# Fused gated cross-attention and routed feed-forward on one core: another order of the first loads and splits, and matmuls without a use where TensorE waits

## The reference

```python
x = x + tanh(g_xattn) * xattn(layernorm(x), ctx, ctx, Wq, Wk, Wv, Wo, bo)   # 16 heads of 16, causal
x = x + tanh(g_ffn) * ffn(layernorm(x), controller, f1, bias, f2)
# xattn: Q = q@Wq.T; K = k@Wk.T; V = v@Wv.T; softmax(mask(Q K^T)/4) V; @Wo.T + bo
# ffn: tokens in groups of 32; logits = grouped @ controller, 32 experts x 4 sets;
#      each (expert, set) takes the one token of its group with the highest logit;
#      relu(token @ f1 + bias) @ f2, and the result goes back to the token it came from
```

## Time and profile before

| | us |
|---|---|
| median of 3 runs | 309.36 |
| lowest, highest | 309.05, 312.26 |
| the profiled execution's own time | 311.98 |
| its span, first to last instruction | 310.3 |
| PE, DVE, ACT, POOL busy in the span | 243.7, 197.7, 168.3, 124.1 |
| mean granted TensorE clock | 0.912 |

### The profile page before, as it was taken

How to read it: one execution, slowest core, us unless ns; L and a number is a source line. 1 busy time by engine, 2 the same in 40 slices (tenths; PEclk the granted TensorE clock), 3 DMA queues, 4 the chain that set the end, 5 groups by cost and what they waited for, 6 DMA issues and landing times.

```text
span 310.3 us, 8572 instructions
## 1 busy us (share of the span) xinstructions
PE 243.7 (79%) x3426; PEld 193.9 (62%) x3426; DVE 197.7 (64%) x433; ACT 168.3 (54%) x345; POOL 124.1 (40%) x230
## 2 busy tenths in 40 slices
PE   0617163798989899898888878698998888789995
PEld 0617052776768687686666656476766777677773
DVE  4574755496859779485777799989995443412222
ACT  1521243485877768485757645336785443334553
POOL 4140233557776767675556665624541000000000
PEclk9985765599999999799989999979999999859999
DMA  6929985647677675738551000049940000001211
GB/s 175 212 92 185 288 167 100 142 109 163 149 178 139 150 162 133 162 65 182 116 138 23 4 4 5 0 145 396 388 161 2 3 4 4 4 2 68 69 68 68
DMA packets 21961, 35.87 MB, mean 116 GB/s; under 512 B 2915, under 2 KB 15779, under 8 KB 20387
## 3 DMA queue, kind: packets, MB, share of 16 engines
q1 hardware_dynamic: 21059, 34.01, 43.1%
q10 hardware_dynamic: 864, 1.33, 1.9%
HBM read 26.65 MB, written 8.39 MB: 113 GB/s over the span
## 4 chain that ended last, share of the span: by engine, by line
PE 27%; POOL 24%; issue 23%; DVE 13%; DMA 7%; ACT 4%; SPq 1%; POOLq 0%; DVEq 0%
POOL pT L377 9%; PE banks L763 7%; PE banks L735 6%; DMA cT<-in_ctxT_dram 6%; PE banks L472 4%; PE banks L772 3%; POOL xs L371 3%; POOL qp L362 3%; POOL kp L362 2%; DVE permb L1144 2%; POOL onl L401 2%; DVE rsum L1099 2%; DVE gmax L1130 1%; PE banks L581 1%; DVE lt L1125 1%
## 5 line engine op out<-in xcount | busy, mean ns | idle before, releaser
L1091 DVE TENSOR_REDUCE nmax<-banks 128x4 f32<-128x512 f32 x64 | 43.7, 685 | 37.5 <-PE banks L535 37.5
L377 POOL TENSOR_SCALAR_AFFINE_SELECT pT<-pT 128x512 f32<-128x512 f32 x64 | 40.7, 637 | 45.4 <-ACT pT L866 45.3
L866 ACT ACTIVATE pT<-banks 128x512 f32<-128x512 f32 x64 | 37.6, 590 | 8.2 <-PE banks L552 7.8
L871 ACT ACTIVATE banks<-cb 128x512 f32<-128x512 bf16 x62 | 37.0, 596 | 5.6 <-DVE nmax L1091 5.5
L581 PE MATMUL banks<-pT,va 128*32 128x128 f32 x512 | 27.7, 289 | 0.8 <-POOL pT L377 0.8
L535 PE MATMUL banks<-kst,qst 96*128 96x128 bf16 x256 | 26.7, 231 | 1.7 <-ACT banks L871 1.4
L1099 DVE RECIPROCAL rsum<-banks 128x256 f32<-128x256 f32 x16 | 28.0, 1748 | 0.0
L552 PE MATMUL banks<-qst,kst 99*128 99x128 bf16 x256 | 25.9, 225 | 1.0 <-ACT pT L866 1.0
L581 PE MATMUL banks<-pT,ones 128*32 128x128 f32 x512 | 26.4, 279 | 0.0
L763 PEld LDWEIGHTS banks<-cf,routed 128*128 128x128 f32 x128 | 21.1, 250 | 7.2 <-issue 6.2
L985 ACT ACTIVATE ys<-banks 128x1024 f32<-128x1024 f32 x16 | 16.7, 1046 | 16.0 <-PE banks L763 16.0
(11 more groups left out here) (115 smaller groups left out, 633.4 us busy)
## 6 DMA issues: line engine op xcount, KB each, us to landing
wx<-in_wexp_dram SPq DMA_DIRECT2D x32, 256.5 KB, 6.8
q_rows<-qp SPq DMA_DIRECT2D x8, 384.0 KB, 2.5
k_rows<-kp SPq DMA_DIRECT2D x8, 384.0 KB, 4.9
qst<-q_rows SPq DMA_DIRECT2D x8, 384.0 KB, 4.7
kst<-k_rows SPq DMA_DIRECT2D x8, 384.0 KB, 4.8
cT<-in_ctxT_dram SPq DMA_DIRECT2D x8, 256.0 KB, 6.7
qst<-q_rows SPq DMA_DIRECT2D x8, 256.0 KB, 5.5
kst<-k_rows SPq DMA_DIRECT2D x8, 256.0 KB, 5.6
```

The source lines that it names most:

```text
L377: pool.affine_select(p, p, [[0, HC], [1, P]], ALU.is_ge, 0.0, base=0, channel_multiplier=-1)\
L866: act.activation(pT[:, n % PR, :], BT[n % 2], ACT.Exp, scale=float(D) ** -0.5).then_inc(p_ready, 1)
L871: act.activation(BS[n % 2], causal, ACT.Copy).then_inc(mask_placed, 1)
L1091: dve.tensor_reduce(nmax[:, b % 2, :].rearrange("p (e j o) -> p e o j", e=2, o=KH)[:, e, o], BS[n % 2].rearrange("p (j t) -> p j t", j=HC) ...
```

## The change

It changes the order of the fill on all engines, and adds 25 matmuls whose result is never read.

- SP: x of 0-1 and 2-3 first, then context pairs 0, 1 and 2 (pair 2 waits for its buffer, that is for `context_low(0)`), V (from ACT's queue), x of 4-7, the shift rows; keys ahead of queries; gates (from ACT's queue) and context pair 3 behind the stacks of pair 0; keep and stack of pair 1; then x of 8-11, WO (from ACT's queue), x of 12-15, the rest of the constants and the controller.
- ACT: loads the identity alone, K and Q; high part of K ahead of the context; context pair 2 and V ahead of `xT_high(1)`; WO's high part in slot 3 of the loop.
- POOL: low part of K (new `weight_low_by_dim`); all three `context_low` ahead of the first `low_part`; WO's low part in slot 4; the controller's copy in slot 56.
- DVE: statistics and `rstd` of four sequences at once; no low part of K; the low part of query pair 0 (new `q_low_first`).
- PE: `keep_warm(9)` ahead of the first transposes and `keep_warm(16)` ahead of the loop.

```diff
--- before.py
+++ after.py
@@ -45,7 +45,7 @@
 LA = 10
 SLOTS_N = 4 * NB + 17
 PARTS = 3
-XL = ((0, 2), (2, 4), (4, 8), (8, 16))
+XL = ((0, 2), (2, 4), (4, 8), (8, 12), (12, 16))
 SROWS = 6 * D
 TROWS = SROWS + PARTS
 STACKS = 4
@@ -145,6 +145,7 @@
 
 
         x_loaded = [sem(f"x_loaded{i}") for i in range(len(XL))]
+        ident_loaded = sem("ident_loaded")
         consts_loaded = sem("consts_loaded")
         masks_ready = sem("masks_ready")
         small_loaded = sem("small_loaded")
@@ -295,24 +296,29 @@
                 stack(kst, k_rows, g, ((0, 3), (1, 3), (2, 3)), k_kept, k_stacked[g % STACKS])
 
             load_x(0)
+            load_x(1)
             load_context(0)
+            load_context(1)
+            load_context(2)
+            sp.dma_start(w[:, V], wattn[:, V]).then_inc(w_loaded[V], 16)
+            load_x(2)
             sp.wait_ge(shift_ready, 1)
             sp.dma_start(kst[SROWS:TROWS].rearrange("p s h b c -> p (s h) (b c)"),
                          shift[:, None, :].to_broadcast([PARTS, STACKS * H, 2 * P])).then_inc(shift_stacked, 16)
-            load_x(1)
-            load_context(1)
-            load_x(2)
+            keep_k(0)
             keep_q(0)
-            keep_k(0)
+            stack_k(0)
             stack_q(0)
-            stack_k(0)
+            sp.dma_start(gb[:, :], gbo).then_inc(gates_loaded, 16)
+            load_context(3)
+            keep_k(1)
+            keep_q(1)
+            stack_k(1)
+            stack_q(1)
             load_x(3)
-            load_context(2)
-            keep_q(1)
-            keep_k(1)
-            stack_q(1)
-            stack_k(1)
-            load_context(3)
+            sp.dma_start(w[:, WO], wattn[:, WO]).then_inc(w_loaded[WO], 16)
+            load_x(4)
+            sp.dma_start(cf[:, P:], constf[:, P:]).then_inc(consts_loaded, 16)
             sp.dma_start(ctrl_in[:, :, :], ctrl).then_inc(small_loaded, 16)
             for g in range(NG2 + 1):
                 if g >= 1:
@@ -365,6 +371,14 @@
                 pool.wait_ge(w_high, m + 1)
                 pool.tensor_tensor(wl[:, m], w[:, m], wh[:, m].bitcast(F32), ALU.subtract).then_inc(w_low[m], 1)
 
+            def weight_low_by_dim(m):
+                pool.wait_ge(w_high, 1)
+                for j in range(2 * KH):
+                    out, high = [t[:, m].rearrange("p k (o d h) -> p (k o) d h", o=KH, d=D)[:, j] for t in (wl, wh)]
+                    last = pool.tensor_tensor(out, w[:, m].rearrange("p k (o h d) -> p (k o) d h", o=KH, d=D)[:, j],
+                                              high.bitcast(F32), ALU.subtract)
+                last.then_inc(w_low[m], 1)
+
             def bias_x(b):
 
                 pool.wait_ge(xn_ready, b + 1)
@@ -411,20 +425,15 @@
                 pool.wait_ge(perm_ready, b + 1)
                 pool.tensor_copy(permT[:, b, :], pc[:, k, :]).then_inc(permT_kept, 1)
 
-            pool.wait_ge(consts_loaded, 16)
+            pool.wait_ge(ident_loaded, 16)
             pool.tensor_copy(identb, ident).then_inc(masks_ready, 1)
-            context_low(0)
-            low_part(qp, 2, qr, 1, 0, qm_ready, ql_ready)
+            weight_low_by_dim(K)
+            for g in range(3):
+                context_low(g)
             low_part(kp, 0, kr, 1, 0, km_ready, kl_ready)
-            context_low(1)
+            weight_low(V)
+            low_part(kp, 0, kr, 1, 1, km_ready, kl_ready)
             low_part(qp, 2, qr, 1, 1, qm_ready, ql_ready)
-            low_part(kp, 0, kr, 1, 1, km_ready, kl_ready)
-            context_low(2)
-            weight_low(V)
-            pool.wait_ge(small_loaded, 16)
-            pool.tensor_copy(ctrl_sb[:, :, :].rearrange("p h (s e) -> p h s e", s=NS),
-                             ctrl_in[:, :, :].rearrange("p h (e s) -> p h s e", s=NS)).then_inc(ctrl_ready, 1)
-            weight_low(WO)
             for n in range(SLOTS_N):
                 s, g = n % 8, n // 8
                 if s % 4 == 0 and 0 <= n // 4 - 1 < NB:
@@ -437,10 +446,16 @@
                     low_part(qp, 2, qr, 1, g + 1, qm_ready, ql_ready)
                 if s == 3 and g + 2 < NG2:
                     low_part(kp, 0, kr, 1, g + 2, km_ready, kl_ready)
+                if n == 4:
+                    weight_low(WO)
                 if s % 4 == 2 and n // 4 < NB:
                     if n == 2:
                         pool.wait_ge(bo_ready, 1)
                     bias_x(n // 4)
+                if n == CH - 8:
+                    pool.wait_ge(small_loaded, 16)
+                    pool.tensor_copy(ctrl_sb[:, :, :].rearrange("p h (s e) -> p h s e", s=NS),
+                                     ctrl_in[:, :, :].rearrange("p h (e s) -> p h s e", s=NS)).then_inc(ctrl_ready, 1)
                 if s == 5 and g + 3 < NG2:
                     context_low(g + 3)
                 if n in (CH + 7, CH + 9, CH + 11):
@@ -608,7 +623,14 @@
                     pe.wait_ge(pm_ready, b - 1)
                 pe.transpose(BP[b % 2][:, 0:P], pc[:, b % 2, :], ident).then_inc(pm_done, 1)
 
-            pe.wait_ge(consts_loaded, 16)
+            def keep_warm(times):
+
+                for _ in range(times):
+                    pe.matmul(bank[1], identb, causal, start=True, stop=True)
+
+            pe.wait_ge(masks_ready, 3)
+            keep_warm(9)
+            pe.wait_ge(ident_loaded, 16)
             transpose_x(0, BB)
             pe.wait_ge(w_low[K], 1)
             for o in range(KH):
@@ -622,7 +644,7 @@
             for o in range(KH):
                 project_q(1, o, bank[2])
 
-            pe.wait_ge(masks_ready, 3)
+            keep_warm(16)
             pe.wait_ge(ones_ready, 2)
             pe.wait_ge(shift_stacked, 16)
             for n in range(SLOTS_N):
@@ -785,15 +807,12 @@
 
         @block.scalar
         def _(act):
-            act.dma_start(cf[:, :], constf).then_inc(consts_loaded, 16)
-            for i in range(2):
+            act.dma_start(ident, constf[:, 0:P]).then_inc(ident_loaded, 16)
+            for i in (K, Q):
                 act.dma_start(w[:, i], wattn[:, i]).then_inc(w_loaded[i], 16)
 
             act.wait_ge(act_warm, 1)
             act.activation(warm[:, :], warm[:, :], ACT.Exp)
-            for i in range(2, 4):
-                act.dma_start(w[:, i], wattn[:, i]).then_inc(w_loaded[i], 16)
-            act.dma_start(gb[:, :], gbo).then_inc(gates_loaded, 16)
 
             def context_high(g):
                 act.wait_ge(ctx_loaded[g % 2], 16 * (g // 2 + 1))
@@ -894,25 +913,24 @@
                 act.activation(rT[:, :, :], bank[0][:, 0:E].rearrange("p (h t) -> p h t", h=KH), ACT.Copy)\
                     .then_inc(rT_ready, 1)
 
+            weight_high(K)
             context_high(0)
-            weight_high(K)
             weight_high(Q)
             xT_high(0, BB)
+            context_high(1)
             k_high(0)
+            k_mid(0)
             q_high(0, bank[4])
             q_mid(0)
-            k_mid(0)
-            context_high(1)
+            context_high(2)
+            weight_high(V)
             xT_high(1, bank[3])
             k_high(1, bank[5])
+            k_mid(1)
             q_high(1, bank[2])
             q_mid(1)
-            k_mid(1)
-            context_high(2)
-            weight_high(V)
             act.wait_ge(gates_loaded, 16)
             act.activation(tg[:, :], gates_sb[:, :], ACT.Tanh).then_inc(tanh_ready, 1)
-            weight_high(WO)
             for n in range(SLOTS_N):
                 s, g = n % 8, n // 8
                 if 1 <= n < CH - 1:
@@ -931,6 +949,8 @@
                     k_high(g + 2)
                 if s == 2 and g + 2 < NG2:
                     k_mid(g + 2)
+                if n == 3:
+                    weight_high(WO)
                 if s == 4 and g + 3 < NG2:
                     context_high(g + 3)
                 if s == 6 and g + 2 < NG2:
@@ -1077,6 +1097,10 @@
                     dve.wait_ge(ql_ready, g)
                 dve.tensor_tensor(qr[:, :], of, qp[:, 0, :], ALU.subtract).then_inc(qr_ready, 1)
 
+            def q_low_first():
+                dve.wait_ge(qm_ready, 1)
+                dve.tensor_tensor(qp[:, 2, :], qr[:, :], qp[:, 1, :], ALU.subtract).then_inc(ql_ready, 1)
+
             def xT_low(g, of=BA):
 
                 dve.wait_ge(xTh_ready, g + 1)
@@ -1144,17 +1168,16 @@
                 dve.tensor_tensor(permb[:, b % 2, :, :], bank[(2, 7)[b % 2]][:, None, 0:P].to_broadcast([P, NG, P]),
                                   groupmask[:, :, None].to_broadcast([P, NG, P]), ALU.mult).then_inc(pm_ready, 1)
 
-            rstd_rows(0, 2)
+            rstd_rows(0, 4)
             normalize_x(0)
             normalize_x(1)
-            weight_low(K)
             weight_low(Q)
             xT_low(0, BB)
+            normalize_x(2)
+            normalize_x(3)
             k_rest(0)
             q_rest(0, bank[4])
-            rstd_rows(2, 4)
-            normalize_x(2)
-            normalize_x(3)
+            q_low_first()
             xT_low(1, bank[3])
```

(1 more changed line is left out.)

## The result

| us | before | changed |
|---|---|---|
| median (range, runs) | 310.77 (309.05 to 312.26, 4) | **319.74** (315.78 to 322.7, 4) |
| profiled execution, span | 311.98, 310.3 | 320.74, 319.0 |
| mean granted clock | 0.912 | 0.875 |

The ratio is 1.0251, 95% interval 1.0166 to 1.0337. Forecast were 309.0 and a range of 305.4 to 312.6, so the time lies 7 us outside.

The account below looks back on a forecast made before the run. It took the loss to be in the fill, in waits for DMAs and POOL. 4.7 us in, 5.03 out, 5.63 out, some 6 in, and the clock's share: slot 8 0.3 earlier, 309.0 against 309.36, range 305.4 to 312.6.

Parts of the forecast that it names:

- Part 1: Fill up to the first scores: the stacks of pair 0 land at 39.0 us against 34.3, 4.7 us later.
- Part 2: From the stacks of pair 0 to slot 8: WO lands at 54.5, slot 8 starts at 61.1 us against 61.42.
- Part 3: The rest: both keep_warm bursts lie in PE's waits and work added to the loop is hidden, 0 us.
- I give it 0: Clock effect of keep_warm(16): none carried to slot 0 or through the wait for WO; 0 us, bounds 0 and -1.9.
- POOL's loop: 0: WO's low part and the controller's copy enter POOL's loop, which has 5.9 us free of 18: 0, at most 0.7.
- from slot 8 ... the change does almost nothing there: From slot 8, first matmul at 61.42 us, the loop repeats and the change does almost nothing.
- a loop from slot 8 to the experts that is off by over 1 us: Sign of being wrong: the loop from slot 8 to the experts, taken as unchanged, longer or shorter by over 1 us.
- Faster: Rival, fill: x of 2-3 lands at 7.0 and the chain runs in POOL's gaps; 305.9 us, chance 0.20.
- Slower by POOL's tiles: Rival, fill: POOL's strided tiles of Wk cost up to 1.27 us each, all 2.8 later; 312.1 us, chance 0.15.
- Clock kept up: Rival, `spread_max(0)` to slot 8: the clock stays up, 18 matmuls take 1.9 us less; 307.1 us, chance 0.08.

## Why the prediction was wrong, and where it was right

**Part 1, late stacks: right, 1.4 us short.** Forecast 39.0, measured 40.40. X of 2-3 landed at 8.66 (8.27), and from the first stack's issue to the last landing it took 11.43 (11.45). K landed at 8.21, not 6.75; its tiles on POOL took 1.93, not 1.6. The rows were ready at 15.15, not 13.8: besides the 1.11 that one tiny instruction took under POOL's 1.26 (1.1 forecast), four more took 0.37 to 0.48 under POOL's four tiles of 0.48, where others of their size took 0.16. Each of the five ends 0.02 to 0.03 us behind the end of a POOL instruction. The Trainium skill, "SBUF — State Buffer", section "Who interferes with whom", states that a DVE instruction with two SBUF inputs contends with a GpSimd instruction that reads SBUF. The rows of L1031, L1033 and L1039 agree; L1029 and L1036 have one tile as input and waited as long, which that section has only for a two-port mode of DVE, and no run shows whether they were in it. I had let the loss act once instead of five times.

**Part 2, the queue behind the stacks: right, and WO 2.2 us short.** WO forecast at 54.5, read at 56.75 behind a wait of 8.43 (6 to 8). The stacks of pair 1 were issued 1 us late (42.08 for 41.1), and the queue from there to x of 8-11 took 13.9 us instead of 12.6. `spread_max(0)` came at 58.46 (56.2), slot 8 at 62.99 (61.1; my own terms add up to 61.2), 4.53 later and not 5.33, since the clock rose at 62. These are mis-sized terms, 1.9 us in all. The reorder alone, which is the change without its matmuls, came out 0.4 above before by the medians of one batch; the forecast for the whole was 0.3 below.

**Part 3: the step that failed.** "keep_warm(9) ... costs nothing" and "I give it 0" are right where I looked: the nine run from 4.57 to 7.98, the sixteen from 27.39 on, both inside waits, and the clock at slot 0 is 0.54. That no clock is carried there holds for this order, with 9.6 us between the sixteen and the scores; on the kernel before, without that gap, it was 0.84. "POOL's loop: 0" is right as well (12.15 of 18 us, before 12.14). But the cost was set to nothing for the whole kernel, with "from slot 8 ... the change does almost nothing there", and in the experts' stage, 180 us behind them, the 25 matmuls cost 8 us: with them 319.74, without 311.64 (in one batch 320.67 with 25 of 32 columns, and 311.64). They do it by the place to which 50 more instructions push the code behind, not by their work: 25 of 32 columns cost as much, 128 nothing that is told. Among its signs of being wrong the prediction has only a loop from slot 8 to the experts that is off by over 1 us. That loop was right (175.68 us, before 176.63); the experts' stage it didn't name at all.

**The rivals.** Faster: transposes came at 15.29, not before 12. Slower by POOL's tiles: 0.48 each, under the 0.7 from which it decides. Clock kept up: no. So the right sign stood in one rival and the right mechanism in none.

**Shown and not shown.** Shown is that the count of added instructions decides, by the place of the code behind (0, 25 and 118 on several fills, 128 on one), that with 25 the clock falls 7 to 12 us into the stage and otherwise after 26 or more, and that ahead of every fall inside the stage stands a second burst that took longer. That PE's stops are waits for a piece of code rests on their timing, 1.2 to 1.7 us behind a packet's end in 33 of 33; no run delays a packet. Argued only is that the longer burst itself drops the clock: the fall follows it after 0.5 us in one kernel and after 6.3 to 7.0 in five, so something else has a part in when it falls. Only instructions ahead of the stage were added, all of them matmuls; another kind on PE, or one on another engine, was not tried. How much of the spread of before's runs (304 to 315) is this clock was not looked into.

## What to carry to other kernels

An instruction added in an idle place can cost far behind it: read the later stages too, above all the granted clock of a stage of many small matmuls, and test an added burst once with its work made tiny and once with another count. Loads that nothing holds back belong ahead of the first dependent transfer in their queue, which gave 2% on the kernel before with its first scores no later (34.38, before 34.69); a chain shared by two pieces of work waits for the later of their inputs.

## What the runs showed of the hardware

- PE's code comes in packets of 16 KB (27 before, 28 changed and with 118 or 128 added matmuls; the other instruction queue keeps its 11). In the experts' stage at full clock one starts every 3.7 to 5.7 us, and the recorded stops, 0.1 to 0.8 us long, end 1.2 to 1.7 us behind a packet's end. From one stop to the next, where neither is hidden, are 248 recorded instructions (255.10 to 259.35 before).
- At 1.2 GHz the experts' pairs leave no gap (PE busy 20.00 of 20 us from 260 to 280, granted clock 0.50), and the clock stays low until the combination. One fall costs 0.9 us for each pair left, so it matters when it comes.
- Early loads hold up a later write in the same queue: from the keys' write to the stacks 3.2 to 4.2 us (three runs) instead of 2.6.
- Four DVE instructions on 128x4 elements took 0.37 to 0.48 us under POOL's of 0.5, and one 1.11 under 1.26, where others of their size took 0.16.
